# Half of the FFN's up projection moved ahead of the second value chunk, and a different set of warm-up matmuls

## What is computed

```python
# x, ctx: [32, 128, 1024] f32; seen by the attention as [4 x 8 rows]; heads 8, head width 16
h = layernorm(x)
q, k, v = Wq @ h + bq, Wk @ ctx + bk, Wv @ ctx + bv
attn = softmax(q . k_window * 16**-0.5)           # 16 keys for each position
x = x + Wo @ (attn . v_window) + bo
h = layernorm(x)
w = top-2 of softmax(h @ gate_w.T), normalised, as a dense [T, 8]
x = x + sum_e w[:, e] * (h @ lora_A[e].T) @ lora_B[e].T     # rank 64, 8 experts -> 512 columns
```

## Time and profile before

| | us |
|---|---|
| median of 3 runs | 1058.51 (1055.99 to 1061.23) |
| the profiled execution, its own time | 1057.9 |
| span of its trace | 1056.1 |
| PE busy | 1011.5 (96%) |
| DVE busy | 872.8 (83%) |
| ACT busy | 582.5 (55%) |
| POOL busy | 432.5 (41%) |

### The profile page before, as it was taken

The page is one execution under the profiler, slowest core; times in us unless marked ns, Lnnn a source line. Parts: engine busy times, 40 slices in busy tenths (PEclk is TensorE's granted clock), DMA queues, the critical chain, the costliest instruction groups (busy, mean ns, idle before and its releaser), DMA issues.

```text
span 1056.1 us, 54652 instructions
## 1 busy us (share of the span) xinstructions
PE 1011.5 (96%) x24508; PEld 869.8 (82%) x24508; DVE 872.8 (83%) x1889; ACT 582.5 (55%) x812; POOL 432.5 (41%) x373
## 2 busy tenths in 40 slices
PE   6879999999999999999999999999999999999987
PEld 5768888888888888888888888888888888888866
DVE  3778888888888888888889888889888888888852
ACT  6666555556555556555555555556555555654420
POOL 7773434434434434343434343444343443443210
PEclk9899999999999999999999999999999999999998
DMA  7232333322333322223332223332233332222210
GB/s 271 78 80 86 83 84 103 103 66 81 82 83 103 103 81 71 76 84 103 103 85 71 84 83 91 103 103 58 87 84 83 103 103 73 76 81 64 64 41 40
DMA packets 157721, 92.47 MB, mean 88 GB/s; under 512 B 139728, under 2 KB 139856, under 8 KB 157520
## 3 DMA queue, kind: packets, MB, share of 16 engines
q1 hardware_dynamic: 157520, 89.25, 28.9%
HBM read 55.16 MB, written 16.78 MB: 68 GB/s over the span
## 4 chain that ended last, share of the span: by engine, by line
PE 87%; issue 5%; DVE 5%; ACT 2%; DMA 1%; POOL 1%; DVEq 0%; SPq 0%
PE bank_a L351 35%; PE bank_b L401 18%; PE bank_c L351 16%; PE bank_b L380 13%; PE bank_a L410 5%; DVE stats L815 1%; DMA raw<-x 1%; DMA prob_t<-ctx 0%; DVE h_sb L875 0%; DVE row_max L886 0%; DVE row_sum L900 0%; DVE pick L861 0%; DVE resid_pair L954 0%; POOL x_split L1120 0%; ACT x_split L688 0%
## 5 line engine op out<-in xcount | busy, mean ns | idle before, releaser
L401 PEld LDWEIGHTS bank_b<-prob_t,v_diag 64*64 64x64 f32 x4608 | 192.0, 134 | 50.3 <-issue 41.9
L401 PE MATMUL bank_b<-prob_t,v_diag 64*64 64x96 f32 (+2 forms) x4608 | 211.4, 239 | 12.6 <-issue 12.2
L351 PE MATMUL bank_a<-down_split,mid_split 128*128 128x264 f32 (+1 forms) x1536 | 213.7, 289 | 1.5 <-DVE mid_split L934 1.4
L351 PEld LDWEIGHTS bank_a<-down_split,mid_split 128*128 128x128 f32 x1536 | 193.4, 188 | 8.6 <-DVE mid_split L934 2.3
L1091 POOL TENSOR_TENSOR prob<-prob,row_inv 128x512 f32<-128x512 f32 x128 | 134.2, 1049 | 159.0 <-DVE row_inv L904 157.2
L351 PE MATMUL bank_a<-up_split,ht_split 128*128 128x512 f32 x768 | 196.6, 407 | 2.8 <-DVE ht_split L941 2.8
L380 PEld LDWEIGHTS bank_b<-k_sb,q_diag 32*32 32x32 f32 x16384 | 155.0, 105 | 43.9 <-issue 36.7
L380 PE MATMUL bank_b<-k_sb,q_diag 32*32 32x32 f32 x16384 | 170.6, 195 | 10.7 <-issue 6.7
L351 PEld LDWEIGHTS bank_a<-up_split,ht_split 128*128 128x128 f32 x768 | 142.8, 192 | 33.7 <-DVE ht_split L941 3.3
L1114 POOL TENSOR_TENSOR attn_split<-attn,attn_split 128x1024 fp32r<-128x1024 f32 x32 | 76.1, 2378 | 145.6 <-ACT attn_split L676 145.6
L913 DVE STREAM_TRANSPOSE prob_t<-prob 128x768 f32<-128x768 f32 x128 | 122.9, 961 | 0.9 <-POOL prob L1091 0.9
(11 more groups left out here) (79 smaller groups left out, 1316.2 us busy)
## 6 DMA issues: line engine op xcount, KB each, us to landing
v_diag<-v_t SPq DMA_DIRECT2D x128, 132.0 KB, 3.3
raw<-x SPq DMA_DIRECT2D x32, 512.0 KB, 4.5
resid_pair<-x SPq DMA_DIRECT2D x32, 512.0 KB, 4.0
out<-resid_pair SPq DMA_DIRECT2D x32, 512.0 KB, 4.3
raw<-ctx SPq DMA_DIRECT2D x30, 512.0 KB, 3.3
stage<-down_w SPq DMA_DIRECT2D x2, 528.0 KB, 10.6
q_diag<-up_w SPq DMA_DIRECT2D x2, 512.0 KB, 5.7
prob_t<-up_w SPq DMA_DIRECT2D x2, 512.0 KB, 7.2
```

The lines of the kernel that those rows point to most:

```text
L351: return nc.tensor.matmul(dst, st[:, s, st_cols], mv[:, m, mv_cols], start=start and n == 0, stop=stop and n == 2)
L401: last = nc.tensor.matmul(bank_b[2 + m % 2][rows, lo * PW:hi * PW], value_blocks(b)[rows, n, :], prob_t[rows, at:at + (hi - lo) * KT], sta ...
```

## The change

Two edits, both on PE alone. In every step that has a `cur`, the first two of the four row blocks of `up(0, e)`, six wide matmuls, stand right after `project_o` and ahead of the second value chunk; with them goes the wait for `ht_lo`. The other two row blocks stay behind the chunk. The warm-up has 62 matmuls of 32x32 instead of 28 of 128x128, all in the same 32 rows and columns.

```diff
                 pe.wait_ge(prob_zero, 1)
                 for n in range(matmuls):
-                    nc.tensor.matmul(bank_c[:, 0:P], prob[:, 0:P], prob[:, 0:P], start=True, stop=True)
+                    nc.tensor.matmul(bank_c[0:KT, 0:KT], prob[:, 0:KT], prob[:, 0:KT], start=True, stop=True)
 
             def head(b0, b1, b2, b3):
 
-                warm_up(28)
+                warm_up(62)
...
                 if cur:
                     project_o(prev, (k_out, ahead.count(1, 1)) if ahead else (v_out, cur.count(1, 1)))
+                pe.wait_ge(ht_lo, old.count(1, 1))
+                for e in range(EK // 2):
+                    up(0, e)
+                if cur:
                     open_weighted(cur, 1)
                     weighted_chunk(cur, 1)
-                pe.wait_ge(ht_lo, old.count(1, 1))
-                for e in range(EK):
+                for e in range(EK // 2, EK):
                     up(0, e)
```

## The result

The changed kernel takes 1075.99 us (median of 4 runs, 1075.04 to 1076.47), the kernel before 1057.86 us beside it (1055.99 to 1061.23). The ratio is 1.0167, with a 95% interval of 1.0139 to 1.0194: slower by 18.1 us. The forecast was 1072 us, within 1061 to 1087.

A forecast was written before the change was run, and what follows sets the result against it. PE was taken as the bound, busy 96%, held by a 13.34 us chain through DVE; 1057.9 + 13.2 (moved wait) + 0 (warm-up's time) + 1 (code seams) = 1072.1 us, range 1061 to 1087.

The forecast's parts named there:

- The chain: From the end of `prev`'s value chunk on PE through ACT, POOL and DVE to `ht_lo`: constant 13.34 us despite PE's stops.
- The moved wait: PE ahead of `up(0)`: waits for `ht_lo` 0.6 to 0.9 us, some 30 times; 0.44 us a step, +13.2 us.
- The split: `up(0)` in two halves around the second value chunk on PE: costs nothing, could save 0.1 us a step.
- The warm-up's time: Head of the kernel on PE: small matmuls take some 6 us; effect on the total 0, bounds -1 and +4 us.
- The warm-up's place: 136 more instructions shift PE's code seams: most stops at record 10 go; +1 us, bounds -5 and +15.
- The sum: PE's step period: 13.34 + 0.05 + 16.99 + 1.51 = 31.89 us against 31.45; total 1072.1 us.
- New stops on the exposed side: Rival: a code seam behind `ht_lo` stops PE 0.5 us each step, adding 15 us: 1087 us; chance 0.20.
- The stops go, and the wait only replaces them: Rival: stop time freed on PE equals the wait, step 31.45 to 31.55 us, total 1058 to 1061 us; chance 0.14.
- The chain getting shorter by itself: Rival: DVE's cast slips ahead of POOL's pass, `ht_lo` about 1 us earlier, total 1038 us; chance 0.06.

The follow-up runs named there:

- the move alone: Changed kernel with the old warm-up of 28 matmuls of 128x128, keeping the moved up projection: 1074.37 us, ratio 1.0171 to the kernel before.
- The wait alone: Kernel before with 62 small warm-up matmuls and only the wait for `ht_lo` ahead of the second value chunk, matmul order kept: 1070.51 us, ratio 1.0071.
- the undivided variant: Changed kernel with all four row blocks of `up(0)` ahead of the second value chunk: 1069.04 us, ratio 1.0120 to the kernel before.
- the warm-up alone: Kernel before with 62 matmuls of 32x32 as its warm-up, up projection not moved: 1045.34 us, ratio 0.9892.

## Why the prediction was right, and what it got wrong

*The chain.* Right. It was 13.34 us in the median of the changed kernel's steps, as in two of the three steps read before the change (13.58 in the third), and the release 0.05 us. That the chain doesn't care for most of PE's stops is shown by the move alone: 9.6 us of stops, a median of 13.34, and 13.74 in the worst step. The reason given, "DVE is not delayed by PE in the chain itself", is too strong. DVE waits in it for PE's `down(0)`, 0.7 us a step, a wait that ends just ahead of the cast whose end goes with POOL's pass (375.31 and 375.29):

```profile
372.40 0.17 DVE L843 COPY logits<-bank_a 128x8 f32<-128x8 f32 x1 [0.67 <-PE bank_a L351]
```

It also reads the bank of `down(1)` for `h_sb`, which PE had finished 2.3 us ahead in this step (378.31, against 380.57 for the start of `h_sb`); so there is room for a stop of 1 us.

*The moved wait.* Right in place and size: some 30 waits were forecast at 0.6 to 0.9 us. The list has 26 between 100 and 1000 us, where 28 steps lie, of 0.73 us on average. The wait alone costs 0.77 us a step against the kernel with the same warm-up. Against the kernel before it is less, since stops in the value chunk had covered part of it; that too was forecast.

*The split.* Wrong, and it is most of what the forecast missed: "Splitting `up(0)` costs nothing that I can see". It costs 0.24 us a step, 7 us over 30 steps, as the undivided variant shows (32.08 against 31.84). I had counted the changes between wide and narrow groups and found as many as before. But each half takes 1.59 us, and half of the undivided 2.95 is 1.48. By the two lengths such a group takes about 0.227 us a matmul and 0.23 us besides, and the split pays the latter once more. The kernel before shows where it sits:

```profile
381.96 3.01 PE L351 MATMUL bank_a<-up_split,ht_split 128*128 128x512 f32 x12
384.81 1.56 PE L351 MATMUL bank_c<-ctx_split,w_split 128*128 128x512 f32 x6
386.30 1.58 PE L401 MATMUL bank_b<-prob_t,v_diag 64*64 64x64 f32 x36
```

`up(1)`, twelve matmuls between a score chunk and another wide group, takes 2.85 us, and the six behind it, ahead of a value chunk, 1.49. So about 0.1 us goes with each side that borders on smaller matmuls, and a group that follows another wide one at once saves it, as the prediction hoped. The first half of the split group doesn't: it takes its 1.59 us behind a wait of 0.1 us as behind one of 0.74. A split with no wait ahead of it was not tried.

*The warm-up's time.* 5.46 us against "some 6": right. The first step comes 1.7 us later, inside the bounds, and I had taken 0. The clock fell to 0.5 of 2.4 GHz (1.2 GHz) in the head again, as in the earlier trace rows, but later: it was still full from 20 to 26 us. What the warm-up has to do with that isn't shown; with the same warm-up and without the move it was at 0.50 in that window. Two windows of the changed kernel (stretch, length, busy time of PE, PEld, DVE, ACT, POOL, granted clock, transfer share, GB/s):

```profile
20.00:26.00 6.00, 1.94 (x204) 1.73 (x190) 4.39 (x10) 2.01 (x3) 2.56 (x3) 1.00 0.05 15
26.00:32.00 6.00, 4.36 (x134) 3.62 (x134) 4.84 (x9) 4.56 (x7) 5.82 (x5) 0.52 0.82 178
```

*The warm-up's place.* Right in kind: the stops moved out of the value chunk, and their going bought nothing while the wait was there. I added 1 us for new stops behind `ht_lo`; there were none. The score chunk in that stretch took 1.28 us on average instead of 1.44, but 1.29 with the move and the old warm-up too, so the place of the seams isn't shown to be the reason. The argument that "stops grew to 1.2 us where transfers were near" was read from a list that doesn't say so: that stop ended at 274.69, and the transfer engines were busy to 3% in the 2.4 us before.

*The sum.* A step was forecast as 13.34 + 0.05 + 16.99 + 1.51 = 31.89 us. Measured, the stretch from the start of `up(0)` to the end of the value chunk of `prev` is 18.70 us on average where 16.99 + 1.51 = 18.50 were forecast, and 13.34 + 0.05 + 18.70 = 32.09 is the mean step of 32.08. The 0.2 us are the split, less 0.05 us in the score chunk, which took 1.34 us in the step that the sum was made from:

```profile
388.83 1.41 PE L380 MATMUL bank_b<-k_sb,q_diag 32*32 32x32 f32 x128
390.17 1.66 PE L351 MATMUL bank_c<-x_split,w_split 128*128 128x512 f32 x6
```

Over 28 steps 0.44 and 0.19 us make 17.6, and the head and tail add 0.4: 18.0 of the 18.1 us. The forecast's 14.2 had 13.2 for 30 steps, nothing for the split, and 1 for stops that did not come. That it was only 3.9 us short is in part luck: that 1 us stood in for a part of the split.

*The rivals.* New stops on the exposed side: not seen. "The stops go, and the wait only replaces them" leant on their being of a size (12.6 and 13.2 us). But the stops inside the chain can't pay for the wait: the warm-up alone gains 1.1%, and nothing on top of the move. The chain getting shorter by itself: not seen; the cast stayed behind POOL's pass. The Trainium skill (Runtime: NRT & Kernel Launch, "Instruction fetch mechanics") says that crossing into the next block is mostly hidden. The prediction took that for a claim that there would be no stops; in the kernel before, 172 packets of code moved between 100 and 1000 us and 23 stops showed, so most were hidden here too. Those that weren't took 12.6 us, and moving the seams by 136 instructions is worth 0.41 us a step.

## What to carry to other kernels

Before moving a wait up on the busiest engine, measure when the thing waited for is ready from the last point at which its chain leaves that engine, in steps with and without other stalls; where the time was the same, as here, the new period could be added up from it (31.89 us forecast, 32.08 measured). Two stalls inside one such interval don't add, and removing one of them may bring nothing: here a gain of 1.1% from the warm-up alone was invisible beside the move. And when an edit changes how many instructions stand ahead of a long unrolled stream, compare against a version with the same number, or the place of the code's seams passes for an effect of the edit.

## What the runs showed of the hardware

- PE ran out of code in a straight stream. One packet of the instruction queue came for each 255 records, and between 100 and 1000 us the stops, up to 1.2 us long, stood at two places of a step: 18 at record 10 of a value chunk, shortly after 64 matmuls of 32x32 that took 1.2 us, and 5 at record 90 of a score chunk. A stop of over 0.25 us ended 1.2 to 1.5 us after a packet of code had landed, and the next packet started 1.0 to 2.1 us after that. 28 and 92 small matmuls in the warm-up had the stops at the same places; 62 had few, nearly all at record 83 of another score chunk.
- An f32 matmul of 32x32 on the same rows and columns as its neighbours took 2 x 5.46/124 = 88 ns on average over the warm-up, where 23 to 26 records fell in a microsecond from 3 to 6 us and 37 from 6 to 7 us; spread over four row groups, as in a score chunk, 1.22/64 = 19 ns.
- A group of wide matmuls between groups of smaller ones carried about 0.23 us beside its matmuls: six took 1.59 us to the start of what follows, twelve 2.95. With another wide group behind it twelve took 2.85, with one ahead of it six took 1.49: about 0.1 us a change.
